# Windowed attention on one core: the inverse roots of the norms taken from VectorE to GpSimd's power

## The reference, cut to what matters

```python
def attn_layer(x, Wqkv, qs, ksc, Wo):
    q, k, v = jnp.split(x @ Wqkv, 3, -1)          # 16 heads of 64
    q, k, v = (sh(q), sh(k), sh(v))
    q = l2norm(q) * qs                            # q / max(|q|, 1e-12), for each head
    k = l2norm(k) * ksc
    q = q * cos * scale + rotate_half(q) * sin * scale
    k = k * cos * inv + rotate_half(k) * sin * inv
    out = local_attention(q, k, v)                # windows of 32, look one window back
    return out.transpose(0, 2, 1, 3).reshape(b, n, INNER) @ Wo

def ffn_layer(x, g, bln, W1, b1, W2, b2):
    mu = x.mean(-1, keepdims=True)
    var = ((x - mu) ** 2).mean(-1, keepdims=True)
    xn = (x - mu) / jnp.sqrt(var + 1e-05) * g + bln
    a, gate = jnp.split(xn @ W1 + b1, 2, -1)
    return a * jax.nn.gelu(gate, approximate=False) @ W2 + b2

for i in range(DEPTH):
    x = attn_layer(shift_tokens(x), ...) + x
    x = ffn_layer(shift_tokens(x), ...) + x
```

## Time and profile before

| | before |
|---|---|
| median of 3 runs | 6063.36 us (6060.19 to 6070.28) |
| span of the profiled execution | 6062.1 us |
| PE busy | 5372.5 us, 89% |
| DVE busy | 4241.2 us, 70% |
| ACT busy | 3913.4 us, 65% |
| POOL busy | 2700.1 us, 45% |

### The profile page before, as it was taken

One profiled execution on the slowest core, in us unless ns is written; L12 is line 12 of the kernel. 1 busy time (PEld: TensorE's weight loads), 2 busy tenths in 40 slices (PEclk: granted clock), 3 DMA queues, 4 the chain that ended last, 5 costly groups with the idle time before them and its releaser, 6 DMA issues. The chain is left out here.

```text
span 6062.1 us, 121575 instructions
## 1 busy us (share of the span) xinstructions
PE 5372.5 (89%) x41154; PEld 3794.5 (63%) x41154; DVE 4241.2 (70%) x16112; ACT 3913.4 (65%) x11510; POOL 2700.1 (45%) x2578
## 2 busy tenths in 40 slices
PE   7885699999999999997489999999999999697989
PEld 5674366666666666665256666666666666464678
DVE  4453688888888888885378888788888887454522
ACT  2211588888888888884178888888888888222333
POOL 0000556556565565652166656566565665230000
PEclk9996799999999999998599999999999999697999
DMA  0000000000000000000000000000000000000000
GB/s 11 22 1 3 22 1 12 9 12 9 1 15 6 12 9 12 8 1 4 21 1 7 10 6 12 9 12 9 4 13 6 12 8 1 5 2 4 2 29 8
DMA packets 30964, 53.45 MB, mean 9 GB/s; under 512 B 7688, under 2 KB 17168, under 8 KB 29712
## 3 DMA queue, kind: packets, MB, share of 16 engines
q1 hardware_dynamic: 30352, 45.66, 2.4%
HBM read 44.60 MB, written 1.05 MB: 8 GB/s over the span
## 5 line engine op out<-in xcount | busy, mean ns | idle before, releaser
L1784 PE MATMUL bank<-wA,next_rowT 128*128 128x512 f32 x2304 | 1213.7, 629 | 194.6 <-DVE turnB L2129 73.1
L1983 ACT ACTIVATE pairs<-pairs,negmax 128x128 f32<-128x128 f32 (+1 forms) x3072 | 1236.8, 418 | 18.6 <-DVE negmax L2090 17.5
L1960 POOL TENSOR_TENSOR turnA<-raw,ropes 128x512 f32<-128x512 f32 x768 | 968.7, 1271 | 169.3 <-ACT raw L2007 140.4
L2090 DVE CUSTOM_DVE_ANT_0 pairs<-bank,bands,big 128x128 f32<-128x128 f32 (+1 forms) x3072 | 941.7, 364 | 64.6 <-PE bank L1716 61.0
L1967 POOL TENSOR_TENSOR qk<-turnA,turnB 128x512 f32<-128x512 f32 x768 | 975.8, 1271 | 0.0
L1944 POOL COPY spread<-recip 128x256 f32<-128x256 f32 x768 | 305.3, 398 | 1257.8 <-DVE recip L2099 1251.4
L1784 PEld LDWEIGHTS bank<-wA,next_rowT 128*128 128x128 f32 x2304 | 369.6, 190 | 676.7 <-DVE turnB L2129 294.3
L1990 ACT ACTIVATE pairsT<-bank 128x512 f32<-128x512 f32 x768 | 465.9, 607 | 302.2 <-PE bank L1729 301.9
L1983 ACT ACTIVATION_READ_ACCUMULATOR pairs<-pairs,negmax 128x1 f32 x3072 | 625.0, 203 | 0.0
L285 POOL TENSOR_TENSOR rstd<-vareps,neg_half 128x2 f32<-128x2 f32 x56 | 39.0, 696 | 1292.4 <-DVE vareps L256 892.7
L2129 DVE TENSOR_TENSOR turnB<-bank,ropes 128x512 f32<-128x512 f32 x768 | 523.1, 681 | 0.0
(11 more groups left out here) (306 smaller groups left out, 11272.8 us busy)
## 6 DMA issues: line engine op xcount, KB each, us to landing
wA<-in_wt_wqkv SPq DMA_DIRECT2D x72, 256.0 KB, 2.8
wB<-in_wt_wo SPq DMA_DIRECT2D x12, 512.0 KB, 3.5
wC<-in_wt_w SPq DMA_DIRECT2D x12, 341.0 KB, 2.9
wD<-in_wt_w SPq DMA_DIRECT2D x12, 192.0 KB, 2.4
big<-in_e_up SPq DMA_DIRECT2D x1, 2048.0 KB
big<-in_e_down SPq DMA_DIRECT2D x1, 2048.0 KB
scl<-in_wt_scales SPq DMA_DIRECT2D x12, 128.0 KB, 3.1
X<-in_x SPq DMA_DIRECT2D x8, 128.0 KB, 2.5
```

What stands on the lines that cost most here:

```text
L1784: pe.matmul(side_bank(i)[:, :], c.next_rowT[:, t * P:(t + 1) * P], wqkv[:, k * 512:(k + 1) * 512], start=True, stop=True).then_inc(s.chunk ...
L1960: g.tensor_tensor(c.turnA[:, m % 2, :].rearrange("p (h d) -> p h d", h=8), c.raw[:, m % 4, :].rearrange("p (h d) -> p h d", h=8), cos, ALU ...
L1983: last = a.activation(tile, tile, ACT.Exp, scale=-1.0, bias=c.negmax[:, 2 * p + side, t:t + 1], accum_out=c.pair_sums[:, p % 4, t, side:si ...
L2090: last = v.tensor_tensor_reduce(c.pairs[:, 2 * (p % 4) + side, AT[t]:AT[t] + SPAN[t]], c.bank[side][:, AT[t]:AT[t] + SPAN[t]], c.bands[:, ...
```

## The change

The Newton chain goes. VectorE now does one instruction for each half of the heads: it takes the maximum of the norms with 1e-24 (a new tile `c.floor`, by `tensor_tensor`, so both inputs are in SBUF) and signals `norms_summed`. GpSimd raises to the power -0.5 in pieces of 16 columns (two token halves by eight heads): "rootk0", "rootq0", "rootk1", "rootq1". The second half's maximum is in slot 5 where its roots were in slot 6. The variance plus epsilon becomes a `tensor_tensor` too, and GpSimd takes its root over two columns after the spread of slot 3 (`pool_ff_root`). `rs_ready` now counts four for each turn. The memset of L2204 goes.

```diff
-DVE_RSQRT_SLOTS = {2: 0, 6: 1}
-POOL_SLOTS = {1: ("cos0", "cos1", "add0"), 2: ("cos2", "add1", "cos3", "add2"), 3: ("add3", "scale0"),
-              4: ("cos4", "cos5", "add4"), 5: ("cos6", "add5", "cos7", "add6"), 6: ("add7", "scale1")}
+DVE_FLOOR_SLOTS = {2: 0, 5: 1}
+POOL_SLOTS = {1: ("cos0", "cos1", "add0"), 2: ("cos2", "add1", "cos3", "add2"), 3: ("add3", "rootk0", "scale0"),
+              4: ("cos4", "cos5", "add4", "rootq0"), 5: ("cos6", "add5", "cos7", "add6"), 6: ("add7", "rootk1", "scale1"),
+              7: ("rootq1",)}
...
+                elif item[:4] == "root":
+                    which = "qk".index(item[4])
+                    g.wait_ge(s.norms_summed, q * 2 + m + 1)
+                    g.tensor_tensor(norms_of(rs[q % 2], m)[:, :, which, :], norms_of(ss, m)[:, :, which, :],
+                                    c.neg_half[:, 0:16].rearrange("p (t h) -> p t h", t=HALVES),
+                                    ALU.pow).then_inc(s.rs_ready, 1)
                 else:
-                    g.wait_ge(s.rs_ready, q * 2 + m + 1)
+                    g.wait_ge(s.rs_ready, q * 4 + 2 * m + 1)
...
+        def pool_ff_root(g, f):
+            g.wait_ge(s.var_ready, f + 1)
+            g.tensor_tensor(ff_rstd, ss[:, ff_var], c.neg_half[:, 0:HALVES], ALU.pow).then_inc(s.rstd_ready, 1)
...
             if p % 4 == 0:
-                v.wait_ge(s.rs_ready, T * 2 + g + 1)
+                v.wait_ge(s.rs_ready, T * 4 + 2 * g + 2)
...
-        def dve_roots(v, x, y):
-            (12 instructions)
...
-            step.after(v.tensor_scalar(ss[:, ff_var], ff_mv[:, :, 1], LN_EPS, None, ALU.add), v)
+            v.tensor_tensor(ss[:, ff_var], ff_mv[:, :, 1], c.floor[:, ff_var], ALU.add).then_inc(s.var_ready, 1)
...
-            if slot in DVE_RSQRT_SLOTS:
-                g = DVE_RSQRT_SLOTS[slot]
+            if slot in DVE_FLOOR_SLOTS:
+                g = DVE_FLOOR_SLOTS[slot]

                 v.wait_ge(s.chunk_rotated, q * ROTATED + 4 * g + 4)
-                if g == 0 and has_turn(q - 3):
-                    dve_roots(v, ss[:, 0:32 + HALVES], rs[q % 2][:, 0:32 + HALVES])
-                else:
-                    dve_roots(v, norms(ss, g), norms(rs[q % 2], g))
-                v.memset(c.recip[:, 0, 31:32], 0.0).then_inc(s.rs_ready, 1)
+                v.tensor_tensor(norms(ss, g), norms(ss, g), c.floor[:, 0:32], ALU.max).then_inc(s.norms_summed, 1)
...
                         pool_spread(g, T, p)
+                        if p == 3 and has_turn(T - 2):
+                            pool_ff_root(g, T - 2)
                         if has_turn(T + 1):
                             pool_prepare(g, T + 1, p)
+                for f in (T1 - 2, T1 - 1):
+                    pool_ff_root(g, f)
```

More of the change, by code:

```diff
@@ L111, in allocate @@
     c.neg_half = sb("neg_half", [P, 64])
+    c.floor = sb("floor", [P, 32 + HALVES])
     c.stats = sb("stats", [P, HALVES, 6])
@@ L196, in _ @@
             v.memset(c.hT[:, :, :], 1.0)
+            v.memset(c.floor[:, 0:32], 1e-24)
+            v.memset(c.floor[:, 32:32 + HALVES], LN_EPS)
             last = v.memset(c.probsT[:, :, :], 0.0)
@@ L1629, in windowed_transformers @@
     w = io[name]
-    names = ("tables_loaded", "tables_ready", "attn_added", "ff_added", "steps",
+    names = ("tables_loaded", "tables_ready", "attn_added", "ff_added", "steps", "norms_summed", "var_ready", "rstd_ready",
              "wo_loaded", "scales_loaded", "ff_loaded", "w2_loaded",
@@ L1638, in windowed_transformers @@
     s = Chip()
-    (tables_loaded, s.tables_ready, s.attn_added, s.ff_added, steps,
+    (tables_loaded, s.tables_ready, s.attn_added, s.ff_added, steps, s.norms_summed, s.var_ready, s.rstd_ready,
      s.wo_loaded, s.scales_loaded, s.ff_loaded, s.w2_loaded,
@@ L1665, in windowed_transformers @@
     rs = (c.big[:, at + 68:at + 136], c.big[:, at + 136:at + 204])
+    ff_rstd = rs[0][:, ff_var]
     ff_stats = c.big[:, at + 204:at + 228].rearrange("p (t k) -> p t k", t=HALVES)[:, :, 0:6]
@@ L2165, in dve_ff_stats, with dve_ff_normalise @@
             step.after(last, v)
-            step.after(v.tensor_scalar(ss[:, ff_var], ff_mv[:, :, 1], LN_EPS, None, ALU.add), v)
-        def dve_ff_normalise(v, f, rstd):
+            v.tensor_tensor(ss[:, ff_var], ff_mv[:, :, 1], c.floor[:, ff_var], ALU.add).then_inc(s.var_ready, 1)
+        def dve_ff_normalise(v, f):
+            v.wait_ge(s.rstd_ready, f + 1)
             for t in range(HALVES):
                 last = v.tensor_scalar(c.xn[:, t, :], ff_bank[:, t * D:(t + 1) * D], ff_mv[:, t, 0:1],
-                                       rstd[:, t:t + 1], ALU.subtract, ALU.mult)
+                                       ff_rstd[:, t:t + 1], ALU.subtract, ALU.mult)
             last.then_inc(s.normed, 1)
@@ L2239, in dve_window @@
                     dve_prepare(v, T + 1, p)
-                elif p == 3:
-                    dve_roots(v, ss[:, ff_var], rs[(T + 1) % 2][:, ff_var])
                 if p == 4 and has_turn(T - 2):
-                    dve_ff_normalise(v, T - 2, rs[(T + 1) % 2][:, ff_var])
+                    dve_ff_normalise(v, T - 2)
                 if p == 7:
@@ L2251, in dve_ff_alone @@
             dve_ff_stats(v, f)
-            dve_roots(v, ss[:, ff_var], rs[0][:, ff_var])
-            dve_ff_normalise(v, f, rs[0][:, ff_var])
+            dve_ff_normalise(v, f)
         def dve_tail(v):
```

## The result

The changed kernel takes 5965.6 us against 6061.8 for the kernel before, a ratio of 0.984 (95% interval 0.9826 to 0.9855). These are medians of four executions; one of the changed kernel's ran at a granted clock of 0.21 and took 22845 us, and the ratio leaves it out (without it the median would be 5964.4 us). The prediction was 5985 us, range 5945 to 6040. Of the page after: the span, the engines' busy time, and the group of the powers (count, busy us, mean ns).

A forecast was written before the change was run, and what follows sets the result against it. TensorE leads, its gaps held open by VectorE's slot-2 roots ahead of the copy of k. Steady turns 79, tables -13, tails 6 and starts 6 make 78 us off the profiled 6062.1: forecast 5985 us, range 5945 to 6040.

The forecast's parts named there:

- Bound and way of the gain: Slot 2's roots delay slot 3's copy of k, which releases chunk 7; chunk 10's wait stays; slot 6's roots gain nothing.
- 0.9 us a turn: Steady turns: the copy of k comes 0.98 us sooner, of which 0.9 arrives; 88 turns give 79 us.
- ScalarE's two gaps: Gaps before the square of chunk 7 and chunk 10's copy let ScalarE come forward 0.54 and 0.35 us, together 0.89.
- A power of 2.9 us and GpSimd's order: GpSimd's 16-column powers take 2.9 us; its 39.3 us a turn fit, with 0.7 (spread 5) and 0.8 (spread 7) to spare.
- L2166's successor: Slot 2's two-column VectorE instruction, now reading two SBUF tiles, is still held until GpSimd's add ends; no gain taken.
- The wait of `dve_tables`, 13 us: VectorE's table instruction, with two SBUF inputs, is held by rootq1: 1.3 us, ten times, 13 us lost.
- The starts, 3 us each: Prologue and first three turns of each run: VectorE loses chains but GpSimd becomes longer; 3 us gained a run, 6 in all.
- TensorE's waits for `spread`: Sign: TensorE never, or hardly, released by `spread`; the prediction falls if `spread` becomes a releaser of TensorE.
- The tails, 3 us each: Tail's two-column roots, 2.38 us alone on the path, become a 0.70 us power and two hand-overs: 6 us for four.
- GpSimd as the bound: Rival: dearer powers make spread 7 late; 6020 us at 3.3 us a power, slower from 3.45; chance 0.18.
- The second rival: No difference: ScalarE, nearly full from chunk 7 to chunk 10, takes up VectorE's shift; 6047 us; chance 0.10.
- The third: Rival: two SBUF inputs do not hold VectorE at L2166's place and the tables, TensorE's gaps close; 5937 us; chance 0.06.

The follow-up runs named there:

- x1: Changed kernel with only slot 2's roots and the variance on GpSimd, the second half's Newton chain back on VectorE in slot 6: 5951.5 us, ratio 0.9823.
- x3: Changed kernel with the feed-forward's normalisation moved from between slot 3's copy of k and chunk 10's rotation to the end of slot 5: 5911.0 us, ratio 0.9757.
- x4: Changed kernel with an extra GpSimd power of two columns (0.70 us) ahead of each of the four roots in a turn: 6083.5 us, ratio 1.0034.
- x5: Changed kernel with four extra VectorE sums over 256 columns (1.31 us together) in slot 2: 6010.2 us, ratio 0.9915.
- x8: Changed kernel with eight extra VectorE sums over 256 columns (2.62 us together) in slot 2: 6130.0 us, ratio 1.0115.
- x7: Changed kernel with a setup-stage probe: small VectorE instructions beside a 64-column GpSimd power and beside two adds of 512 columns; 5998.4 us in one execution.
- x2: Changed kernel with the first half's Newton chain back on VectorE in slot 2, second half's roots and the variance's on GpSimd: 6012.5 us, ratio 0.9923.
- x6: Changed kernel with the edits of x1 and x3 together: 5901.0 us, ratio 0.9743.
- x11: Changed kernel with eight extra VectorE sums (2.62 us) in slot 3, behind the reciprocal and directly ahead of the copy of k: 6048.9 us, ratio 0.998.

## Why the prediction was right, and where it wasn't

**Bound and way of the gain: right.** The copy of k in slot 3 was late because of slot 2's roots, chunk 10 stayed the next wait, and the second half's roots lay where VectorE had time. x1 shows the first and the last, x3 the second: taking 0.64 us off the VectorE work after the copy took 0.64 off the turn.

**0.9 us a turn: right, slightly low.** The turn fell by 0.98 us, which is exactly the 0.98 by which the copy was to come sooner. The cut to 0.89 by ScalarE's two gaps didn't bind: in the changed kernel's turn both gaps are closed, which is 0.43 + 0.35 = 0.78 us, and the other 0.20 came from ScalarE's instructions following each other more closely. The forecast of 79 us for 88 turns became 84 us in the 86 steady ones.

**A power of 2.9 us and GpSimd's order: right.** 2.91 us measured, 38.6 us a turn of 39.3 forecast. The margins were put at 0.7 (spread 5) and 0.8 (spread 7); the trace shows 0.95 and 0.94, the doses 0.97 (x4) and 0.88 (x5, x8).

**L2166's successor: right.** It is held for 1.23 us beside GpSimd's add.

**The wait of `dve_tables`, 13 us: wrong.** VectorE's timeline shows it at 2033.31 for 0.68 us, as before, though rootq1 runs on GpSimd from 2031.61 to 2034.51. Nor was the maximum of slot 5 held (2018.70, 0.19 us) beside rootq0, 2016.50 to 2019.42. So it is in the whole program: all twelve table instructions (L2152) took 681 to 693 ns, ten of them beside a power, and 94 maxima beside rootq0 took 183 to 195 ns. The step that failed was to carry the row of an add of 512 columns over to a power of 16. The length of GpSimd's instruction is not what holds: x7. The same maximum is held where a cosine of 512 columns is what runs on GpSimd, as x2's timeline shows:

```profile
2028.54 1.27 POOL L1966 TENSOR_TENSOR turnA<-raw,ropes 128x512 f32<-128x512 f32 x1
...
2028.65 1.20 DVE L2220 TENSOR_TENSOR big<-big,floor 128x32 f32<-128x32 f32 x1
```

The Trainium skill, in SBUF — State Buffer, section "Who interferes with whom", has a VectorE instruction with two SBUF inputs contend with a GpSimd instruction that reads SBUF, and gives the shared ports to whoever comes first for the whole instruction. The runs agree for adds and cosines (1.2 us) and disagree for powers (0.1 us of 10.57); here the measurement decides.

**The starts, 3 us each: wrong, +0.5 each.** Two windows of the first start, before and after, and TensorE's timeline after (turn markers L1770, and the waits for `spread`):

```profile
660.00:720.00 60.00, 45.41 (x257) 26.56 (x257) 47.47 (x165) 37.27 (x119) 39.34 (x36) 0.86 0.00 1
```

```profile
660.00:720.00 60.00, 45.04 (x260) 26.27 (x260) 36.86 (x134) 39.29 (x124) 58.31 (x43) 0.88 0.00 1
```

```profile
678.96 0.69 PE L1770 MATMUL bank<-ident,Y 128*128 128x128 f32 x2
...
717.50 0.44 PE L1743 MATMUL bank<-ident,spread 128*128 128x128 f32 x2 [2.63 <-POOL spread L1949]
...
723.92 0.44 PE L1743 MATMUL bank<-ident,spread 128*128 128x128 f32 x2 [1.60 <-POOL spread L1949]
...
724.99 0.44 PE L1770 MATMUL bank<-ident,Y 128*128 128x128 f32 x2
...
765.96 0.44 PE L1743 MATMUL bank<-ident,spread 128*128 128x128 f32 x2 [2.87 <-POOL spread L1949]
```

The prologue did gain: the first turn begins 678.96 - 642.15 = 36.8 us after the run's first turn marker, 7.8 less than the 44.6 before. But GpSimd, busy for 58.3 of 60 us, carries its roots into the first turn, TensorE waits for its spreads, and that turn takes 46.0 us instead of 38.5. In it TensorE waits 4.2 us for spreads and, at its beginning, 3.7 us for keys that GpSimd has still to scale; in the kernel before it waited 1.8 us for a spread there and for no keys. The prediction saw that GpSimd's work is longer than this turn and still put a gain there; its lower bound, a loss of 8 us for both, would have covered it. TensorE's waits for `spread`, which the prediction named as a sign of its fall, are 13.0 us in the whole program, and all of them over 0.1 us lie in these starts. That GpSimd's load is the cause is supported by x1 and x2: with one half of the roots each, their starts are 164.6 and 159.9 us against 169.0, and their first turns 39.9 and 38.0 us.

**The tails, 3 us each: right in kind.** 2.1 and 4.1 us. Each root left an idle time of 0.81 us ahead of L2175 where a chain of 2.38 us was the earlier trace rows:

```profile
5094.01 0.16 DVE L2170 TENSOR_TENSOR big<-big,floor 128x2 f32<-128x2 f32 x1
5094.99 0.73 DVE L2175 TENSOR_SCALAR xn<-bank,big 128x128 f32<-128x128 f32 x2 [0.81 <-POOL big L1991]
```

**11 us more than the sum: not foreseen, and not the change's own work.** The rest after the second run, before and after:

```profile
5209.00:6062.00 853.00, 720.18 (x7514) 545.32 (x7514) 345.49 (x838) 250.94 (x429) 104.10 (x33) 0.88 0.03 9
```

```profile
5120.00:5962.00 842.00, 709.29 (x7514) 539.39 (x7514) 345.44 (x839) 251.28 (x429) 104.12 (x33) 0.90 0.03 9
```

TensorE does the same 7514 matmuls in 720.2 and in 709.3 us at granted clocks of 0.88 and 0.90. In the profiles of the thirteen kernels it took from 841.8 to 853.2 us (x1 846.1, x2 849.2, x3 847.7, x6 842.1, x11 852.3), each in one execution. The clock accounts for it in the rows. It need not be a matter of the kernel: x11's ten executions alone range from 6040.8 to 6053.3 us, at mean granted clocks of 0.949 and 0.947. Why the clock differs was not settled. Counted without it the measured sum is 89 us; the forecast, less the 13 for the tables and the 6 of the starts, would have been 85.

Of the profiled 100 us, 78 were forecast. The difference of 22 is 5 in the steady turns, 13 for the tables, -7 in the starts and 11 in the rest: that the total came as near as it did is in part luck, since the gain that the starts did not bring hid half of the wait that the tables did not have.

**Rivals.** GpSimd as the bound didn't come about at 2.91 us, but x4 shows its mechanism, its wait and nearly its price. Its point of decision was put at 3.45 us (its own terms, 3e = 1.7, give 3.47); with the margin of 0.97 and the gain of 0.98 as measured it would be about 3.55, an estimate. The one run beyond it agrees: at 3.6 the kernel is 0.3% slower than before. The second rival fell with ScalarE's gaps. The third was right in that the tables are not held, and wrong for L2166's place and for chunk 10.

## What to carry to other kernels

An engine's busy share says whether work fits; whether it may move is a question of two hand-offs: how long after its input comes, and how long before its output is wanted. Measure that margin by a dose, on each way out of the place: the same 1.31 us was free behind a reciprocal and cost 0.43 us a turn ahead of it. And move only what lies ahead of the late hand-off: the half of the roots that had time on its old engine gained nothing in the steady turns, and on top of the first half it cost 4.4 and 4.1 us in the starts.

## What the runs showed of the hardware that I had not expected

A GpSimd power holds VectorE for 0.1 us at its start (x7) and not for its length: not in the first 3.3 us of one of 10.57 us, and not in the later part of those of 2.9 us, where the tables and the maxima of slot 5 lie. Adds and cosines of 512 columns hold one VectorE instruction for their full 1.2 us, with two inputs or, beside the adds of x7, with one. And stages with the same code can differ by 11 us of 850 between two profiled executions, at granted clocks of 0.88 and 0.90: more than most terms of this sum, so a total should be compared stage by stage before its last per mille is explained.
